# Routing four graphs at once in a fused attention and mixture-of-experts layer, with two PSUM banks for V

## The chip, the cores and the metric

The kernel runs on one core of a Trainium2 chip. The metric is the device time of one execution in microseconds, the median of several. TensorE (PE; its weight loads are listed as PEld), VectorE (DVE), ScalarE (ACT), GpSimd (POOL) and SyncE (SP) each work through their own instructions in order and wait for each other by semaphores; DMAs are issued on SP's, ACT's and POOL's queues.

## The reference

64 graphs of 128 nodes and 512 features each go through one layer: attention with 16 heads and the doubled adjacency as bias, then a mixture of 8 experts of which each node takes its two best.

```python
x = x + attention(layernorm(x), adj, adj, Wq, Wk, Wv, Wo)      # 16 heads, softmax(q k / sqrt(512) + 2 adj) v, Wo
h = layernorm(x)
scores = maximum(h @ gate_W + gate_b, EPS)                      # (64, 128, 8)
p = softmax(scores);  idx = top_k(p, 2)
w = maximum(p, 0.1);  comb = where(in_top_k, w / sum(w[idx]), 0)
y = einsum('bsd,edf->bsef', h, expert_W) + expert_b
x = x + einsum('bsef,bse->bsf', y, comb) / 2
```

## The kernel before

Everything is float32. Projections are made of three matmuls of a rounded high part and the rest as a low part (`three`, L454): high with high, high with low, low with high.

**First phase** (`phase_a`). Loops on all engines run over turns t = -6 to 71 and, in each, over quarters c = 0 to 3. In turn t the attention scores of graph t are made, probabilities of graph t - 1 are transposed, graph t - 2 is multiplied by its values, and graph t - 3 (with t - 2 in odd turns) gets its output projection, residual and second norm. TensorE also makes one big unit of 24 matmuls per quarter (`big`): in even turns Q, Q, V, V for the next pair of graphs, in odd turns O, K, O, K. Units alternate between the banks ps_p[0] and ps_p[1]; V and O have a second, wide half of 264 columns (256 of the projection and 8 gate scores), which goes to ps_g for V (`G_V`) and to ps_m for O (`G_O`). A unit waits until the one before it in its bank has been read: K and Q by VectorE's low parts (L802, L804), V by ScalarE (L654 to L659, which also writes gate_x), O by VectorE's residual (L857 to L859).

**Routing** is made for two graphs at a time, all on 8-element rows, in a chain of small VectorE instructions in which each waits for the one before (`link`): `gate_scores` (turn odd, c = 2), `choose` (odd, c = 3; the two best experts of each node), then in the even turn at c = 1 `weigh` (the weights) and `find_places` (the row of each expert's list that a node gets). Between them TensorE counts nodes with three small matmuls into a corner of ps_g (`G_P`, L595 to L597, even turn, c = 1). Since V's wide half starts the same bank anew, the first V unit of the turn waits for find_places' second instruction (L960, which writes fill). GpSimd then scatters the normalised rows (xn2, four buffers) into the experts' lists x_lists by two indirect DMAs a graph (L1156), one graph a turn, and has the Newton steps of 1/sqrt (`second_rstd`, L1101 to L1111) and the normalising of the probabilities (L1146).

**Transition.** SP loads the experts' weights from turn 61 on, ScalarE rounds them (L755), and VectorE subtracts to get their low parts (`expert_lo`, L974, four instructions of 512 columns for each expert): six at the places of LO_AT between turns 64 and 67, two after the table. The table (L1046 to L1069) lists for each of 135 tiles its expert and its rows, from the counts in fill. All engines meet at the end of the phase.

**Second phase** (`phase_b`): for each tile ScalarE's queue loads 128 rows (L1288), TensorE transposes them and multiplies by the expert's weights (L1260 to L1262), VectorE makes the low part (L1300), adds the bias and scales, and GpSimd adds the rows into out by an indirect DMA (L1343).

## Time and profile before

| | us |
|---|---|
| median of 3 runs (lowest, highest) | 1661.66 (1660.23, 1663.96) |
| the profiled execution | 1662.81 |
| its span in the trace | 1661.0 |
| PE busy, PEld busy | 1550.8, 1410.9 |
| DVE, ACT, POOL busy | 1215.8, 955.9, 974.0 |

The first phase takes the first 1193 us or so, the second the rest. A line of a timeline gives start, duration, engine, line of the kernel, instruction, tile written<-tiles read, shape and count; in brackets stands how long the engine was idle before it and what it was waiting for.

### The profile page before, as it was taken

Reading aid. Unit: us, or ns where it says so; the run is one execution under the profiler, and the core shown is the slowest. Engines: PE = TensorE matmul, PEld = TensorE weight load, DVE = VectorE, ACT = ScalarE, POOL = GpSimd, SP = SyncE. Lnnn points to the kernel's source line nnn. Section 1 sums busy time; section 2 is a strip of 40 time slices with the busy share of each in tenths; the row PEclk is TensorE's granted clock in tenths of the full one; section 3 lists DMA queues with packets and bytes.
Section 4 is the critical chain, followed back from the end, with each engine's and each line's share of the span. In section 5 each row is a group of like instructions: output and inputs, shape, how many; then the busy total and the mean of one; then the engine's idle time right before and its main releaser. Section 6 shows DMA issues by size and latency. Waiting matters only on the chain. (4 is left out here: it accounts for less than half of the span.)

```text
span 1661.0 us, 45460 instructions
## 1 busy us (share of the span) xinstructions
PE 1550.8 (93%) x12808; PEld 1410.9 (85%) x12808; DVE 1215.8 (73%) x4952; ACT 955.9 (58%) x3129; POOL 974.0 (59%) x1788
## 2 busy tenths in 40 slices
PE   6999999999999999999999999966189999999996
PEld 6999999999999999999999999955167777777775
DVE  5578888888888888888888788877745555555554
ACT  4687777777777777777777777775111111111111
POOL 3255666566666666566665666556235565565655
PEclk9999999999999999999999999977599999999998
DMA  6787988789888888888887888794658898898886
GB/s 226 194 233 199 257 241 241 237 248 253 246 241 240 244 247 239 237 239 247 228 244 225 246 233 228 221 293 142 217 102 158 168 174 164 162 169 165 164 160 106
DMA packets 188629, 351.98 MB, mean 212 GB/s; under 512 B 20960, under 2 KB 30304, under 8 KB 188256
## 3 DMA queue, kind: packets, MB, share of 16 engines
q1 hardware_dynamic: 135520, 238.47, 51.7%
q0 software_dynamic: 29680, 69.55, 21.6%
q10 hardware_dynamic: 23184, 41.05, 8.0%
q8 instruction: 109, 1.79, 0.5%
q14 instruction: 136, 1.11, 0.2%
HBM read 189.48 MB, written 159.52 MB: 210 GB/s over the span
## 5 line engine op out<-in xcount | busy, mean ns | idle before, releaser
L678 ACT ACTIVATE prob<-prob,nmax 128x128 f32<-128x128 f32 x1024 | 398.8, 395 | 175.3 <-DVE amax L833 168.8
L1146 POOL TENSOR_TENSOR prob<-prob,rinv 128x512 f32<-128x512 f32 x256 | 261.4, 1042 | 241.3 <-DVE rinv L850 241.2
L829 DVE CUSTOM_DVE_ANT_0 prob<-ps_s,bias 128x128 f32<-128x128 f32 x1024 | 237.7, 287 | 142.1 <-PE ps_s L530 106.5
L1343 POOL DMA_INDIRECT out<-yt,token x135 | 211.6, 1567 | 196.3 <-DMA out<-yt,token 72.3
L1281 ACT ACTIVATE xgT_hi<-ps_x 128x512 fp32r<-128x512 f32 x135 | 80.7, 598 | 386.8 <-PE ps_x L1266 339.4
L1260 PE MATMUL ps_y<-we,xgT_hi 128*128 x540 | 260.8, 483 | 5.8 <-DVE xgT_lo L1300 5.8
L1261 PE MATMUL ps_y<-we,xgT_hi 128*128 x540 | 214.8, 398 | 0.0
L1262 PE MATMUL ps_y<-we,xgT_lo 128*128 x540 | 214.0, 396 | 0.0
L678 ACT ACTIVATION_READ_ACCUMULATOR prob<-prob,nmax 128x1 f32 x1024 | 196.7, 192 | 0.0
L833 DVE TENSOR_REDUCE amax<-prob 128x4 f32<-128x512 f32 x256 | 175.6, 686 | 8.9
L539 PE MATMUL ps_t<-const,prob 128*128 128x128 f32 x1024 | 164.8, 284 | 15.2 <-ACT pT L716 12.1
L1300 DVE TENSOR_TENSOR xgT_lo<-ps_x,xgT_hi 128x512 fp32r<-128x512 f32 x135 | 93.2, 690 | 105.6 <-ACT xgT_hi L1281 102.4
L1266 PE MATMUL ps_x<-const,xg 128*128 128x128 f32 x540 | 147.5, 276 | 21.1 <-DMA xg<-x_lists 21.1
L1156 POOL DMA_INDIRECT x_lists<-xn,pos x128 | 133.6, 1044 | 43.5 <-issue 37.7
L716 ACT ACTIVATE pT<-ps_t 128x512 f32<-128x512 f32 x256 | 152.1, 594 | 11.9 <-PE ps_t L539 9.7
L455 PE MATMUL ps_p<-xT_hi,wk_hi 128*128 128x256 f32 x512 | 150.9, 295 | 1.8 <-DVE xT_lo L815 1.8
L530 PE MATMUL ps_s<-ks,qs 96*128 96x128 f32 x1024 | 145.8, 265 | 7.2 <-issue 4.9
L1260 PEld LDWEIGHTS ps_y<-we,xgT_hi 128*128 128x128 f32 x540 | 102.7, 190 | 56.3 <-issue 9.3
L455 PE MATMUL ps_p<-xT_hi,wq_hi 128*128 128x256 f32 x512 | 149.7, 292 | 0.6 <-DVE kT_lo L802 0.6
L456 PE MATMUL ps_p<-xT_lo,wk_hi 128*128 128x256 f32 x512 | 145.8, 285 | 0.0
L457 PE MATMUL ps_p<-xT_hi,wk_lo 128*128 128x256 f32 x512 | 145.7, 285 | 0.0
L530 PEld LDWEIGHTS ps_s<-ks,qs 96*128 96x128 f32 x1024 | 138.7, 193 | 7.9 <-issue 7.7
(191 smaller groups left out, 4770.4 us busy)
## 6 DMA issues: line engine op xcount, KB each, us to landing
ks<-kq_parts SPq DMA_DIRECT2D x192, 256.0 KB, 4.2
qs<-kq_parts SPq DMA_DIRECT2D x192, 256.0 KB, 6.3
xg<-x_lists ACTq DMA_DIRECT2D x135, 260.5 KB
xin<-x SPq DMA_DIRECT2D x64, 256.0 KB, 7.2
kq_parts<-kT_hi SPq DMA_DIRECT2D x32, 512.0 KB, 3.8
kq_parts<-kT_lo SPq DMA_DIRECT2D x32, 512.0 KB, 4.8
kq_parts<-qT_hi SPq DMA_DIRECT2D x32, 512.0 KB
kq_parts<-qT_lo SPq DMA_DIRECT2D x32, 512.0 KB
```

The source lines that it names most:

```text
L455: mm(out_, lhs_hi, rhs_hi, start=first, stop=False)
L530: last = mm(ps_s[c % 2][:, P * h:P * h + P], qs[:, r, h, c, :], ks[:, r, h, c, :], start=True, stop=True)
L539: last = nc.tensor.transpose(ps_t[:, P * h:P * h + P], prob[:, b % 2, c, h, :], ident)
L678: last = nc.scalar.activation(prob[:, r, c, h, :], prob[:, r, c, h, :], ACT.Exp, bias=nmax[:, r, i:i + 1], scale=-1.0, accum_out=rsum[:, r ...
L716: nc.scalar.activation(pT[:, c].rearrange("p h t -> p (h t)"), ps_t[:, :], ACT.Copy).then_inc(pT_done, 1)
L829: last = nc.vector.tensor_tensor_reduce(out=prob[:, r, c, h, :], in0=ps_s[c % 2][:, P * h:P * h + P], in1=bias[:, b % 4, :], scale=-1.0, s ...
L833: nc.vector.tensor_reduce(amax[:, r, HC * c:HC * c + HC], prob[:, r, c, :, :], axis=AX.X, op=ALU.max, apply_absolute_value=True).then_inc( ...
L1146: tt(prob[:, r, q], prob[:, r, q], rinv[:, r, HC * q:HC * q + HC].unsqueeze(2).to_broadcast([P, HC, P]), ALU.mult)\
L1260: nc.tensor.matmul(ps_y[r][:, :], xgT_hi[:, r, c, :], hi, start=c == 0, stop=False)
L1261: nc.tensor.matmul(ps_y[r][:, :], xgT_hi[:, r, c, :], lo, start=False, stop=False)
L1262: last = nc.tensor.matmul(ps_y[r][:, :], xgT_lo[:, r, c, :], hi, start=False, stop=c == DC - 1)
L1343: pool.indirect_dma_start(out=out, out_offset=bass.IndirectOffsetOnAxis(ap=token[:, m, :], axis=0), in_=yt[:, r, :], in_offset=None, compu ...
```

## The change

Routing works on groups: fourteen of four graphs (0 to 55), then four of two (56 to 63). All its tiles grow from two to four graphs. The steps move: with `last` the last graph of the group, gate_scores at turn last + 3, c = 3; choose at last + 4, c = 0; ScalarE's exponential at last + 4, c = 1; the counting matmuls (`places`) and weigh at last + 4, c = 2; `combine` (the end of the old weigh) and find_places at last + 5, c = 0. For groups of four last + 3 is even. The two V units get a bank each: the first puts its wide half into ps_o, between the multiplications by v of two turns, the second into ps_g. xn2 has eight buffers instead of four, gate_x six instead of eight, and all_one lies in xn2. The products of Wo with the gate move from ps_o to ps_t, and with them a wait from the first multiplication by v to the first transposes of probabilities. Scatters come two turns later for groups of four; so in turns 62 and 63 two graphs each are scattered. Of the experts' low parts four stand in the last turns, two behind the table, and two in the second phase behind the second tile's low part; a table row first_need tells TensorE for the first three tiles which low parts it must wait for.

```diff
+LATE = 6
+GROUPS = [(4 * q, 4) for q in range((B - 8) // 4)] + [(b, 2) for b in range(B - 8, B, 2)]
+LAST_OF = {b + n - 1: g for g, (b, n) in enumerate(GROUPS)}
...
-        G_V, G_P = ps_g[:, 0:D // 2 + E], ps_g[:, 3 * P:3 * P + 3 * E]
+        G_V, G_P = [ps_o[:, 0:D // 2 + E], ps_g[:, 0:D // 2 + E]], ps_g[:, 3 * P:3 * P + 5 * E]
-        O_W, O_S = ps_o[:, 0:DC * E], ps_o[:, DC * E:DC * E + E]
+        O_W, O_S = ps_t[:, 0:DC * E], ps_t[:, DC * E:DC * E + E]
...
-        LO_AT = {0: (B, 0), 1: (B, 2), 2: (B + 1, 0), 3: (B + 2, 0), 4: (B + 2, 2), 5: (B + 3, 0)}
+        LO_AT = {0: (B, 0), 1: (B, 2), 2: (B + 1, 0), 3: (B + 2, 0)}
...
-                    if 2 * n + part:
-                        pe.wait_ge(v_done, 2 * n + part)
-                    if part == 0 and okp((t - 6) // 2):
-                        pe.wait_ge(place_step, PLACE * ((t - 6) // 2) + 1)
+                    if part == 0 and ok(t - 2):
+                        pe.wait_ge(oT_done, t - 1)
+                    if part == 1 and n >= 1:
+                        pe.wait_ge(v_done, 2 * n)
+                    if part == 1 and t - 5 in LAST_OF:
+                        pe.wait_ge(place_step, PLACE * LAST_OF[t - 5] + 1)
...
+                    if b % 2 and ok(b + 3):
+                        pe.wait_ge(v_done, b + 4)
...
+            def places(g):
+                first, n = GROUPS[g]
+                pe.wait_ge(route_step, ROUTE * g + 16)
+                pe.wait_ge(v_done, min(B, first + n + 6))
+                if g >= 1:
+                    pe.wait_ge(place_step, PLACE * (g - 1) + 1)
...
+                mm(rows(G_P, 0, n + 1), tri[:, :], rows(sums, 0, n + 1), start=True, stop=False)
+                for i in range(1, n):
+                    mm(rows(G_P, i + 1, n + 1), ones[:, :], rows(sums, 1, n + 1 - i), start=False, stop=False)
+                for i in range(n):
+                    last = mm(rows(G_P, 0, 1), ones[:, :], rows(sums, i + 1, i + 2), start=False, stop=i == n - 1)
...
-                if b >= 4:
-                    act.wait_ge(scattered[b % 4], 32 * (b // 4))
+                if b >= 8:
+                    act.wait_ge(scattered[b % 8], 32 * (b // 8))
...
-                    p = (t - 6) // 2
-                    if not odd and okp(p):
-                        if c == 1:
-                            weigh(p)
-                            find_places(p)
-                    p = (t - 5) // 2
-                    if odd and okp(p):
-                        if c == 2:
-                            gate_scores(p)
-                        if c == 3:
-                            choose(p)
+                    if c == 3 and t - 3 in LAST_OF:
+                        gate_scores(LAST_OF[t - 3])
+                    if c == 0 and t - 4 in LAST_OF:
+                        choose(LAST_OF[t - 4])
+                    if c == 2 and t - 4 in LAST_OF:
+                        weigh(LAST_OF[t - 4])
+                    if c == 0 and t - 5 in LAST_OF:
+                        combine(LAST_OF[t - 5])
+                        find_places(LAST_OF[t - 5])
...
+            ts(first_need[:, :], tab_f[:, 0, 0:RING], float(DC), float(DC), ALU.mult, ALU.add)
...
-            for e in range(len(LO_AT), E):
+            for e in range(len(LO_AT), LATE):
                 expert_lo(e)
...
-                    if c == (3 - 2 * a if t < B else 3) and okp(p):
-                        scatter(p, a)
+                    if c == (3 if t >= B or not odd else 1):
+                        for b in range(B):
+                            g, a = GROUP_OF[b]
+                            if t == GROUPS[g][0] + GROUPS[g][1] + 4 + a:
+                                scatter(b)
...
+                        if not t.after(R):
+                            need = pe.value_load(v["first_need"][0:1, bass.ds(t.count(), 1)], min_val=DC, max_val=DC * E)
+                            pe.wait_ge(v["we_lo_done"], need)
...
+                    if (g, j) == (0, 0):
+                        for e in range(LATE, E):
+                            for i in range(DC):
+                                hi, lo = (we[:, (2 * e + part) * DC * D + D * i:(2 * e + part) * DC * D + D * i + D] for part in range(2))
+                                tt(lo, lo.bitcast(f32), hi.bitcast(f32), ALU.subtract).then_inc(v["we_lo_done"], 1)
```

The order of three places, with the semaphores that an instruction waits for. First TensorE at the first V unit of turn 34, where the halves meet (ps_p the first half, ps_g or ps_o the wide one), before:

```order
L455 MATMUL ps_p<-wv_hi,xT_hi 128x256
L456 MATMUL ps_p<-wv_lo,xT_hi 128x256
L457 MATMUL ps_p<-wv_hi,xT_lo 128x256
L455 MATMUL ps_g<-wv_hi,xT_hi 128x264 [waits place_step,v_done]
L456 MATMUL ps_g<-wv_lo,xT_hi 128x264
L457 MATMUL ps_g<-wv_hi,xT_lo 128x264
```

and after:

```order
L466 MATMUL ps_p<-wv_hi,xT_hi 128x256
L467 MATMUL ps_p<-wv_lo,xT_hi 128x256
L468 MATMUL ps_p<-wv_hi,xT_lo 128x256
L466 MATMUL ps_o<-wv_hi,xT_hi 128x264 [waits oT_done]
L467 MATMUL ps_o<-wv_lo,xT_hi 128x264
L468 MATMUL ps_o<-wv_hi,xT_lo 128x264
```

The wide half has left the bank that the counts lie in, and waits for oT_done instead of place_step and v_done; place_step is now waited for by the second V unit of every other even turn.

Second, VectorE in turn 34 from the end of quarter 1 (amax is the last instruction of the maxima; qT_lo and xT_lo are low parts; den and what follows is weigh), before:

```order
L833 TENSOR_REDUCE amax<-prob 128x4 [waits s_read]
L804 SCALAR_TENSOR_TENSOR qT_lo<-ps_p,qT_hi 128x256 [waits q_hi_done]
L804 SCALAR_TENSOR_TENSOR qT_lo<-ps_p,qT_hi 128x256
L815 TENSOR_TENSOR xT_lo<-ps_m,xT_hi 128x512 [waits xT_hi_done]
L928 TENSOR_REDUCE den<-eexp 128x2 [waits gexp_done]
L929 TENSOR_TENSOR em<-eexp,mask 128x16
L930 RECIPROCAL wgt<-den 128x2 [waits route_step]
L931 TENSOR_REDUCE e<-em 128x2
```

and after:

```order
L859 TENSOR_REDUCE amax<-prob 128x4 [waits s_read]
L830 SCALAR_TENSOR_TENSOR qT_lo<-ps_p,qT_hi 128x256 [waits q_hi_done]
L830 SCALAR_TENSOR_TENSOR qT_lo<-ps_p,qT_hi 128x256
L841 TENSOR_TENSOR xT_lo<-ps_m,xT_hi 128x512 [waits xT_hi_done]
L855 ISA prob,nmax<-ps_s,bias 128x128 [waits pT_full,s_full]
L855 ISA nmax 128x1
```

Behind xT_lo came the 18 instructions of weigh and find_places; now the maxima of quarter 2 (ISA prob,nmax) follow at once.

Third, VectorE in turns 66 and 67 (pos is the end of find_places for graphs 60 and 61, we the experts' low parts, score the start of the last routing), before:

```order
L964 TENSOR_REDUCE posf<-place_k 128x4 [waits place_step]
L968 CAST pos<-posf 128x4 [waits scattered1,scattered0,place_step]
L974 TENSOR_TENSOR we<-we 128x512 [waits we_hi_done,place_step]
L974 TENSOR_TENSOR we<-we 128x512 x3
L974 TENSOR_TENSOR we<-we 128x512 [waits we_hi_done]
L974 TENSOR_TENSOR we<-we 128x512 x3
L884 SCALAR_TENSOR_TENSOR score<-gate_sum,shift,gate_x 128x8 [waits rstd2_step]
```

and after:

```order
L984 TENSOR_REDUCE posf<-place_k 128x2x2 [waits place_step]
L988 CAST pos<-posf 128x2x2 [waits scattered6,scattered5,scattered7,scattered4,place_step]
L994 TENSOR_TENSOR we<-we 128x512 [waits we_hi_done,place_step]
L994 TENSOR_TENSOR we<-we 128x512 x3
L915 SCALAR_TENSOR_TENSOR score<-gate_sum,shift,gate_x 128x8 [waits rstd2_step]
```

The low parts of two experts stood between the end of find_places and the last scores; one expert's is left there.

## Rows read from the trace of the kernel before

**Rows 1.** Stretches: us, busy of PE, PEld, DVE, ACT, POOL, clock, DMA.
```profile
400.00:600.00 200.00, 199.01 (x1952) 192.58 (x1951) 167.63 (x820) 157.10 (x550) 130.93 (x258) 1.00 0.87 249
...
1185.00:1190.00 5.00, 0.00 (x0) 0.00 (x0) 4.76 (x12) 0.00 (x0) 0.00 (x0) 0.50 1.03 325
```

**Rows 2.** Timeline (start us, us, engine): first V matmul, turns 2, 4, 8, 58.
```profile
86.83 0.36 PE L455 MATMUL ps_p<-wv_hi,xT_hi 128*128 128x256 f32 x1
...
119.84 0.36 PE L455 MATMUL ps_p<-wv_hi,xT_hi 128*128 128x256 f32 x1
...
188.75 0.36 PE L455 MATMUL ps_p<-wv_hi,xT_hi 128*128 128x256 f32 x1
...
1043.06 0.36 PE L455 MATMUL ps_p<-wv_hi,xT_hi 128*128 128x256 f32 x1
```

**Rows 3.** Timeline, TensorE's weight loads at the two V units of turn 34.
```profile
634.13 0.19 PEld L456 LDWEIGHTS ps_p<-wv_lo,xT_hi 128*128 128x128 f32 x1
...
634.26 0.19 PEld L457 LDWEIGHTS ps_p<-wv_hi,xT_lo 128*128 128x128 f32 x1
...
634.54 0.19 PEld L455 LDWEIGHTS ps_g<-wv_hi,xT_hi 128*128 128x128 f32 x1
...
637.73 0.19 PEld L455 LDWEIGHTS ps_p<-wv_hi,xT_hi 128*128 128x128 f32 x1 [0.38 <-DVE qT_lo L804]
...
639.44 0.19 PEld L455 LDWEIGHTS ps_g<-wv_hi,xT_hi 128*128 128x128 f32 x1 [0.24 <-ACT gate_x L659]
```

**Rows 4.** Timeline, VectorE in turn 34: routing, then the low part of q.
```profile
631.72 0.16 DVE L928 TENSOR_REDUCE den<-eexp 128x2 f32<-128x16 f32 x1
...
634.27 0.15 DVE L960 TENSOR_TENSOR fill<-ps_g,fill 128x8 f32<-128x8 f32 x1
...
636.93 0.74 DVE L804 SCALAR_TENSOR_TENSOR qT_lo<-ps_p,qT_hi 128x256 fp32r<-128x256 f32 x2
```

**Rows 5.** Timeline, ScalarE in turn 34: first exponential of quarter 2.
```profile
637.05 0.40 ACT L678 ACTIVATE prob<-prob,nmax 128x128 f32<-128x128 f32 x1 [2.82 <-DVE amax L833]
```

**Rows 6.** Timeline, VectorE: choice (turn 33), residual and scores (turn 35).
```profile
623.78 0.14 DVE L904 TENSOR_TENSOR eq<-score,m 128x16 f32<-128x16 f32 x1
...
625.82 0.21 DVE L916 TENSOR_TENSOR mask_sum<-mask 128x16 bf16<-128x16 f32 x1
...
646.62 0.29 DVE L829 CUSTOM_DVE_ANT_0 prob<-ps_s,bias 128x128 f32<-128x128 f32 x1 [2.42 <-PE ps_s L530]
...
648.85 0.16 DVE L859 TENSOR_TENSOR gate_x<-ps_m,gate_x 128x8 f32<-128x8 f32 x1
...
652.89 0.36 DVE L884 SCALAR_TENSOR_TENSOR score<-gate_sum,shift,gate_x 128x8 f32<-128x8 f32 x2
...
654.11 0.18 DVE L893 TENSOR_TENSOR dlt<-score,m 128x16 f32<-128x16 f32 x1
```

**Rows 7.** Timeline, TensorE in turn 35: first matmul of the second O unit.
```profile
650.39 0.36 PE L455 MATMUL ps_p<-wo_hi,oT_hi 128*128 128x256 f32 x1
```

**Rows 8.** Timeline, VectorE from the last routing into the second phase.
```profile
1167.42 4.91 DVE L974 TENSOR_TENSOR we<-we 128x512 fp32r<-128x512 f32 x8
...
1172.25 0.36 DVE L884 SCALAR_TENSOR_TENSOR score<-gate_sum,shift,gate_x 128x8 f32<-128x8 f32 x2
...
1179.11 0.16 DVE L1032 CAST ends<-fill 1x8 int32<-1x8 f32 x1
...
1206.97 0.69 DVE L1300 TENSOR_TENSOR xgT_lo<-ps_x,xgT_hi 128x512 fp32r<-128x512 f32 x1 [5.63 <-ACT xgT_hi L1281]
```

**Rows 9.** Timeline, GpSimd: a scatter in turn 63, the last rstd2 in turn 66.
```profile
1128.23 1.01 POOL L1156 DMA_INDIRECT x_lists<-xn,pos  x1 [0.15 <-issue]
...
1162.11 0.59 POOL L1107 TENSOR_TENSOR nwt<-var,rstd 128x1 f32<-128x1 f32 x1 [0.18 <-POOL rstd L1106]
...
1164.68 0.19 POOL L1111 TENSOR_TENSOR off<-nmu,rstd 128x1 f32<-128x1 f32 x1 [0.18 <-POOL rstd L1110]
```

**Rows 10.** Timeline, ScalarE's queue: first loads of the second phase.
```profile
1194.29 4.61 ACTq L1288 DMA_DIRECT2D xg<-x_lists  x5
```

More of the change, by code:

```diff
@@ L886, in gate_scores @@
                 link(last)
-                for r in range(2):
+                for r in range(n):
                     last = nc.vector.scalar_tensor_tensor(out=score[:, r, :], in0=score[:, r, :], scalar=rstd2[:, k + r:k + r + 1],
@@ L946, in find_places @@
-            def find_places(p):
-                step = [0]
-                def link(ins):
-                    step[0] += 1
-                    ins.then_inc(place_step, 1)
-                    dve.wait_ge(place_step, PLACE * p + step[0])
-                r = p % 2
-                old, new = fill[:, r, :], fill[:, 1 - r, :]
-                places = G_P.rearrange("p (a e) -> p a e", a=3)
-                dve.wait_ge(place_full, p + 1)
-                tt(place[:, :, :], places[:, 0:2, :], old.unsqueeze(1).to_broadcast([P, 2, E]), ALU.add)
-                link(tt(new, places[:, 2, :], old, ALU.add))
+                link(ts(score[:, 0:n, :], score[:, 0:n, :], GATE_EPS, None, ALU.max))
@@ new lines, in landed, with combine @@
+            def landed(graphs):
+                for b in graphs:
+                    dve.wait_ge(scattered[b % 8], 32 * (b // 8 + 1))
+            def combine(g):
+                first, n = GROUPS[g]
+                link = chain(ROUTE * g, 22, route_step)
+                link(nc.vector.scalar_tensor_tensor(out=wgt[:, :, 0:n], in0=wgt[:, :, 0:n], scalar=1.0 / K,
+                                                    in1=wtot[:, 0:n].unsqueeze(1).to_broadcast([P, K, n]), op0=ALU.mult, op1=ALU.mult))
+                link(tt(comb_k[:, :, 0:n, :], mask[:, :, 0:n, :], wgt[:, :, 0:n].unsqueeze(3).to_broadcast([P, K, n, E]), ALU.mult))
+                landed(range(max(0, first - 8), first - 8 + n))
+                k = first % 8
+                tt(xn2[:, k:k + n, D + 1:W], comb_k[:, 0, 0:n], comb_k[:, 1, 0:n], ALU.add)
+                link(nc.vector.tensor_copy(xn2[:, k:k + n, D], const[:, C_TOK + first:C_TOK + first + n]))
@@ new lines, in find_places @@
+            def find_places(g):
+                _, n = GROUPS[g]
+                link = chain(PLACE * g, 0, place_step)
+                r = g % 3
+                old, new = fill[:, g % 2, :], fill[:, 1 - g % 2, :]
+                places = G_P.rearrange("p (a e) -> p a e", a=5)
+                dve.wait_ge(place_full, g + 1)
+                tt(place[:, 0:n, :], places[:, 1:n + 1, :], old.unsqueeze(1).to_broadcast([P, n, E]), ALU.add)
+                link(tt(new, places[:, 0, :], old, ALU.add))
@@ L961, in find_places @@
                 for k in range(K):
-                    last = tt(place_k[:, k], place[:, :, :], mask[:, k], ALU.mult)
+                    last = tt(place_k[:, k, 0:n], place[:, 0:n, :], mask[:, k, 0:n], ALU.mult)
                 link(last)
-                link(nc.vector.tensor_reduce(posf[:, :, :], place_k[:, :, :, :], axis=AX.X, op=ALU.add))
-                if p >= 2:
-                    for a in range(2):
-                        dve.wait_ge(scattered[2 * (p % 2) + a], 32 * (p // 2))
-                link(nc.vector.tensor_copy(pos[:, r], posf[:, :, :]))
+                link(nc.vector.tensor_reduce(posf[:, :, 0:n], place_k[:, :, 0:n, :], axis=AX.X, op=ALU.add))
@@ L970, in expert_lo @@
+                if g >= 3:
+                    before, m = GROUPS[g - 3]
+                    landed(range(before, before + m))
+                link(nc.vector.tensor_copy(pos[:, r, :, 0:n], posf[:, :, 0:n]))
             def expert_lo(e):
@@ L1195, in _ @@
                         first_rstd(p)
-            for k in range(4):
-                pool.wait_ge(scattered[k], 32 * (B // 4))
+            for k in range(8):
+                pool.wait_ge(scattered[k], 32 * (B // 8))
 def phase_b(nc, v):
```

199 lines of the change are left out of this document (94 added, 105 removed).

## The prediction

> **What bounds the kernel now.** I read the stretches first. Between 400 and 600 us TensorE is busy 199.0 of 200 us at the full clock, while VectorE has 167.6 and ScalarE 157.1 [rows 1]. So the first phase runs at TensorE's pace, and only what stops its stream is worth time. Matmul ends are modelled, so a short stop hardly shows in the busy share; the starts show it. The reader is to take the same matmul, the first of a V unit, pair after pair [rows 2]. Before the first routing a pair of graphs takes 119.84 - 86.83 = 33.01 us. With routing, 25 pairs take 1043.06 - 188.75 = 854.31 us, that is 34.17 each: 1.16 us more.
>
> TensorE's own rows tell where those 1.16 us go [rows 3]. Inside a unit weight loads follow each other by 0.12 to 0.13 us (634.13 to 634.26). At the wide half of the first V unit the step is 634.54 - 634.26 = 0.28. The second V unit starts late, idle 0.38 until VectorE's low part of q; its wide half is idle 0.24 until ScalarE has read gate_x. VectorE's rows say why [rows 4]: weighing and placing of a pair begin at 631.72, the fill count that TensorE awaits is written at 634.27, and the low part of q, queued behind, comes at 636.93. ScalarE's exponentials start 2.82 us late for the same reason [rows 5], and its read of V stands behind them. So one lump of routing on VectorE, at quarter 1 of every even turn, causes all three stops.
>
> At the end of the first phase VectorE is the bound: it subtracts for two experts from 1167.42, starts the last routing at 1172.25, counts the fill at 1179.11, builds the table, subtracts for two more experts, and the second phase's first loads are issued at 1194.29 [rows 8, 10]. After that TensorE has the say again, and the change leaves that part as it is.
>
> **Term 1, the stops in the pairs.** Each V unit of a pair now has a bank of its own, so the wide half of the second waits for a read of the pair before. The fill that frees G_P is written at quarter 0 and wanted at quarter 3, three units of 24 matmuls at 0.12 us (2.9 us each) later. And quarter 1 of the even turn carries no routing at all. What should stay of the 1.16 us is the cost of the placing matmuls. I add up what is lost at the V units over the 28 pairs from turn 6 on, each start less the same step in turns 2 and 4, where there is no routing yet: wide half of the first 5.1 us and the step behind it 2.2, start of the second 12.0, its wide half 5.2 and behind it 2.9, together 27.4 us or 0.98 per pair. The two ways agree if the remaining 0.18 of the 1.16 is the placing matmuls and the restart behind them. I take 27.
>
> Waits that are already met should cost nothing: the same wide half of V with the same wait on v_done, in turns 2 and 4, is within those 33.01 us.
>
> **Term 2, matmuls added.** Fourteen groups of four issue 8 small matmuls, four groups of two issue 4: 128 instead of 96. Before, three of them with the restart cost at most the 0.18 us a pair left over above; If one more costs 0.03 us (an estimate from that 0.18, most of which is the restart), it is 14 x 0.33 + 4 x 0.21 = 5.5 us against 32 x 0.18 = 5.8: nothing. Were each of the 32 more a full weight step of 0.12 [rows 3], it would be 4 us, the other end of the bound. The Trainium skill (TensorE: Matmul & The Clock Gate, on small matmuls) states a floor of about 25 ns from start to start, which would give the same sum.
>
> **Term 3, where VectorE's routing lands now.** Choosing costs 625.82 + 0.21 - 623.78 = 2.25 us and scores 1.40 for two graphs [rows 6]. A column costs (0.61 - 0.18) / (512 - 16) = 0.9 ns, by the low parts of two experts (4.91 us for 8, [rows 8]) and the last score link [rows 6], so 16 more are 0.015 us a link. Four graphs make the choice about 2.4 and the scores, with four instructions more of 0.18, about 2.15. Scores go to quarter 3 of an even turn, choosing to quarter 0 of the next. There the maximum of quarter 1 stood idle 2.42 us for TensorE [rows 6]: the choice fits in almost exactly. Scores push quarter 0 about 0.8 us later. Behind stands the residual, whose last read is 648.85 + 0.16 = 649.01, and TensorE wants that bank at 650.39 [rows 6, 7]: 1.4 us of room less 0.8 leaves 0.4 to 0.6. So I cost it at 0 to 0.5 us a group of four, 0 to 7 us in all, and take 1. Weighing (8 links of 2.25 / 11 = 0.2, 1.6 us) falls at quarter 2 of odd turns, where scores of 1.40 stood before.
>
> The wait for gate_sum moves to the first transposes of probabilities, one turn earlier; a whole V unit of TensorE lies between, and the price is 0. Scatters keep one graph a turn, two turns later, and xn2 has eight buffers for it.
>
> **Term 4, the transition.** Only four low parts stay in front of the last routing. It waits then for the last rstd2, 1164.68 + 0.19 [rows 9], instead of 1172.25: up to 7.3 us earlier. The table has one more instruction, 0.2 us. Two low parts stand behind it as before. The last two go behind the second tile of the second phase, where VectorE idles until 1206.97 and needs 8 x 0.61 = 4.9 us [rows 8]: hidden. Padding is the rival for the end of the phase; DMA is full from 1185 to 1190 [rows 1], but padding is issued on the fill count, which moves as well. Against the 7.1 us: the two graphs' delay of the scatters is caught up in turns 62 and 63, each with two more indirect DMAs of 1.01 us on GpSimd [rows 9], ahead of the rstd and the last normalising. Some of it lies in GpSimd's idle time; I take 1 us, bounds 0 and 2. Two of these also come while keys of the last graph are awaited from full DMA queues: 0 to 1.6 us, I take 0.5. And the first two experts' subtractions now run beside GpSimd's last normalising. Beside such a subtraction a small GpSimd instruction took 0.59 us, and 0.19 without [rows 9]; two to four such steps make 0 to 1.5 us, I take 0.6. Left: 5 us, bounds 2 and 7.
>
> The Trainium skill (SBUF — State Buffer, on the shared port pair) states that a VectorE instruction with two SBUF inputs locks GpSimd out for its whole length, and that descriptors of GpSimd's DMAs can starve. That speaks against low parts in the second phase. By it each of GpSimd's instructions there would wait up to one 0.61 us subtraction. The trace bears the rule out: the 0.59 against 0.19 us of [rows 9] is of that size, but GpSimd has nothing queued between the first tiles' token copies and the first scatter-add, so the sum stays the same.
>
> **Sum.** 27 - 1 + 5 = 31 us. Against the profiled execution (1662.81 us, of which 1661.0 is span) that is 1631.8; the median of the runs shown, 1661.66, is 1.15 lower, and from it comes 1630.7. I say 1630.5.
>
> **Rivals.** (a) The residual comes late in the turns with a choice, by 0.5 to 1 us in each of 14 groups: 7 to 14 us back, 1637 to 1644. For it: room of half a microsecond only, estimated. Against: VectorE is early in that turn, since quarter 1 before it is empty. (b) The transition gives nothing, since GpSimd's doubled scatters or the DMA queues end last: 1635.5. For it: DMA at its full share in two stretches. Against: every one of them starts on something that also moves. (c) The change doesn't do what it says: TensorE's stops come from the wait as such, and a wide half with two waits stays at 0.28. Then 10 to 15 us stay, 1641 to 1646. Against: turns 2 and 4. (d) Slower: scores and choice of four graphs, one behind the other on VectorE, hold up residual and maximum so far that TensorE loses over 31 / 14 = 2.2 us in each such group. That needs links of four graphs to cost half as much again (0.3 us instead of 0.2 for 19 links, 1.9 us) and the low part of k, next in the queue, to be late too; at 3 us a group it is 1642 + 30 = about 1672. The 0.9 ns a column worked out above speaks against: it gives 0.02 us, not 0.1.
>
> **Chances.** Forecast 1626 to 1634: 0.60. (a) 0.15. (b) 0.12. (c) 0.07. (d) 0.03. Something unseen that ends within 0.2% (about what a measurement can tell from no change, 3.3 us): 0.03. The range leaves out the upper part of (c) and the tails, and takes in (a) and (b): 1624 to 1643. Faster by over 0.2% is all but (d) and the unseen: 0.94, same 0.03, slower 0.03.
>
> **What would show it.** Right: a pair of graphs takes about 33.2 us, the V units' loads step 0.12 at their wide halves, no row at the second V unit names qT_lo or gate_x; the second phase's first loads come about 31 us earlier than 1194. Term 3 is wrong if TensorE's second O unit of every other odd turn has an idle time put down to VectorE's gate_x. Term 4 is wrong if from the last residual to the first load of the second phase it is still some 36 us. Wrong altogether if 34.2 us a pair stay.

## The result, and the profile after

The changed kernel takes 1675.47 us (median of 4 runs, 1670.76 to 1679.36) against 1662.47 us (4 runs, 1660.23 to 1663.96) for the kernel before, measured beside it: 1.0078 times as long, 95% interval 1.0049 to 1.0107. Forecast were 1630.5 us, with 1624 to 1643 as the range. The change makes the kernel 13 us slower where 31 us faster were forecast.

The profiled execution of the changed kernel took 1670.76 us, the lowest of its four, with a span of 1668.9; so between the two profiles there are 7.9 us of the 13. The stretch from 400 to 600 us first, beside [rows 1]; the columns are the same:

```profile
400.00:600.00 200.00, 194.88 (x1952) 191.19 (x1950) 161.07 (x721) 156.91 (x544) 128.46 (x255) 1.00 0.86 242
```

TensorE is busy 194.9 of 200 us, where it had 199.0. VectorE has less to do than before (161.1 against 167.6), and still TensorE stands more. The first matmul of the V units of turns 2, 6 and 58 (timeline; start us, us, engine), beside [rows 2]:

```profile
86.46 0.37 PE L466 MATMUL ps_p<-wv_hi,xT_hi 128*128 128x256 f32 x1
...
152.61 0.37 PE L466 MATMUL ps_p<-wv_hi,xT_hi 128*128 128x256 f32 x1
...
1056.09 0.37 PE L466 MATMUL ps_p<-wv_hi,xT_hi 128*128 128x256 f32 x1
```

The two unrouted pairs take 66.15 us, as before. From turn 6 to turn 58 it is 903.48 us, 69.50 for each group of four turns; before, two pairs took 68.34. Turn 58 is reached 13.0 us later than in [rows 2]. The pairs alternate: one of each two takes 33.1 us, as if nothing were routed, the other 34.8 to 38.3.

What TensorE waits for between 200 and 1050 us (view of the waits: us in total, times, longest) has two entries that count:

```profile
PE ps_p L466 <- DVE gate_x L885: 17.2, 13, 1.7
PE ps_p L466 <- DVE qT_lo L830: 10.8, 8, 1.8
```

In the kernel before the same view has 3.8 us for qT_lo and 0.3 for the fill count. A group of four turns takes 69.50 us here and 66.5 where TensorE waits for nothing (experiments 3 and 6); over 850 us that makes about 36 us, and the two waits are 28 of them. The first entry is the second O unit of the turn with the choice, which awaits the residual's read of its bank. The second is the first V unit of the next turn, which awaits the low part of q. One group shows both. First the choice in turn 31, on VectorE, beside [rows 6]:

```profile
579.70 0.17 DVE L876 SCALAR_TENSOR_TENSOR rinv<-amax,rinv 128x8 f32<-128x8 f32 x1
579.79 0.18 DVE L929 TENSOR_TENSOR eq<-score,m 128x32 f32<-128x32 f32 x1
...
580.24 0.19 DVE L931 TENSOR_REDUCE kmax<-key 128x4 f32<-128x32 f32 x1
580.46 0.69 DVE L932 TENSOR_TENSOR mask<-key,kmax 128x32 f32<-128x32 f32 x1
581.19 0.97 DVE L933 SCALAR_TENSOR_TENSOR score<-mask,score 128x32 f32<-128x32 f32 x1
582.19 0.19 DVE L934 TENSOR_REDUCE m<-score 128x4 f32<-128x32 f32 x1
582.41 1.00 DVE L935 TENSOR_TENSOR eq<-score,m 128x32 f32<-128x32 f32 x1
583.44 0.33 DVE L936 TENSOR_TENSOR key<-eq,const 128x32 f32<-128x32 f32 x1
...
584.25 0.19 DVE L941 TENSOR_TENSOR mask_sum<-mask 128x32 bf16<-128x32 f32 x1
...
586.89 0.16 DVE L885 TENSOR_TENSOR gate_x<-ps_m,gate_x 128x8 f32<-128x8 f32 x1
```

GpSimd and TensorE at the same time:

```profile
580.05 2.06 POOL L1166 TENSOR_TENSOR prob<-prob,rinv 128x512 f32<-128x512 f32 x2 [0.26 <-DVE rinv L876]
582.07 1.29 POOL L1203 TENSOR_TENSOR oT_lo<-oT,oT_hi 128x512 fp32r<-128x512 f32 x1
583.32 0.40 POOL L1208 TENSOR_TENSOR bias<-bias 128x128 f32<-128x128 f32 x1
...
587.19 0.36 PE L466 MATMUL ps_p<-wo_hi,oT_hi 128*128 128x256 f32 x1 [1.28 <-DVE gate_x L885]
```

The choice spans 579.79 to 584.44, that is 4.65 us; forecast were 2.4. Seven of its eleven instructions take the 0.2 us that were reckoned with. The other four take 0.69, 0.97, 1.00 and 0.33, and each of them ends 0.05 to 0.07 us behind an instruction of GpSimd: 581.15 and 582.16 behind the two products (580.05 + 1.03 = 581.08 and 580.05 + 2.06 = 582.11), 583.41 behind oT_lo (583.36), 583.77 behind the bias (583.72). Reductions, which read one tile, stay at 0.19 in the middle of it, at 582.19. And it is VectorE itself that lets GpSimd go: the products are released by the rinv at 579.70, the instruction just ahead of the choice.

The kernel before has one such meeting too, in the routing of turn 34, between the rows of [rows 4]. An instruction of weighing, whose neighbours take 0.15 to 0.17 us, takes 0.58 and ends at 632.38, behind GpSimd's subtraction (632.34):

```profile
631.80 0.58 DVE L929 TENSOR_TENSOR em<-eexp,mask 128x16 f32<-128x16 f32 x1
...
631.04 1.30 POOL L1183 TENSOR_TENSOR oT_lo<-oT,oT_hi 128x512 fp32r<-128x512 f32 x1
```

Second, placing in turn 32 on VectorE, and TensorE's first V unit:

```profile
599.44 1.95 DVE L982 TENSOR_TENSOR place_k<-place,mask 128x32 f32<-128x32 f32 x2
601.43 0.22 DVE L984 TENSOR_REDUCE posf<-place_k 128x8 f32<-128x64 f32 x1
601.68 0.94 DVE L988 CAST pos<-posf 128x8 int32<-128x8 f32 x1
...
605.38 0.39 PE L466 MATMUL ps_p<-wv_hi,xT_hi 128*128 128x256 f32 x1 [1.43 <-DVE qT_lo L830]
```

GpSimd has the same products from 599.31 on for 2.04 us and oT_lo from 601.31 for 1.29. Combining and placing span 598.35 to 602.62, 4.27 us; so it is, within 3.9 to 4.3 us, in twelve of the fourteen groups of four.

The transition went as forecast. The fill count is cast at 1186.73 and the first loads go out at 1202.04:

```profile
1186.73 0.16 DVE L1050 CAST ends<-fill 1x8 int32<-1x8 f32 x1
...
1202.04 3.55 ACTq L1313 DMA_DIRECT2D xg<-x_lists  x4
```

From the first V matmul of turn 58 to the cast it is 130.64 us against 136.05 ([rows 2, 8]), and to the first loads 145.95 against 151.23 ([rows 2, 10]), 5.3 us less.

### The profile page after: what moved, and what is told of

Its sections match the earlier page's. It is cut to its first block and busy times, and to the rows that moved or that the text cites. A ratio compares the mean times of both kernels' runs of the same rounds, so it can differ in the third digit from the quotient of the medians.

```text
span 1668.9 us, 45005 instructions
## 1 busy us (share of the span) xinstructions
PE 1540.0 (92%) x12840; PEld 1412.7 (85%) x12840; DVE 1203.5 (72%) x4505; ACT 966.3 (58%) x3115; POOL 973.4 (58%) x1788
## 3 DMA queue, kind: packets, MB, share of 16 engines
q14 instruction: 132, 1.08, 0.2%
## 5 line engine op out<-in xcount | busy, mean ns | idle before, releaser
L555 PE MATMUL ps_t<-const,prob 128*128 128x128 f32 x1024 | 164.9, 284 | 15.7 <-ACT pT L741 10.1
L1339 DVE TENSOR_TENSOR yt<-ps_y,e_bias 128x512 f32<-128x512 f32 x135 | 93.4, 692 | 72.0 <-DMA out<-yt,token 45.9
```

Source lines behind the costliest of these rows:

```text
L555: last = nc.tensor.transpose(ps_t[:, P * h:P * h + P], prob[:, b % 2, c, h, :], ident)
```

## The experiments

Each quoted passage is what was expected, written down before the run. **Theory A**: VectorE's instructions with two operands in SBUF stand while a tensor_tensor of GpSimd runs, so the choice and the placing cost about twice their bare length where the change puts them, and TensorE pays. **Theory B**: four graphs at once are simply too long a lump for these quarters. **Theory C**: it is the order on VectorE, not GpSimd. All times below are medians; the difference is to the kernel before on the same chip, and in brackets stand the ratio of the two and its 95% interval. Waits are TensorE's between 200 and 1050 us, from one profiled execution of each kernel.

**1. The choice ahead of the step that releases GpSimd.** In the same quarter, two steps change places:

```
+                    if c == 0 and t - 4 in LAST_OF:
+                        choose(LAST_OF[t - 4])
                     if c == 0 and ok(t - 1):
                         inverse_sums(t - 1, 1)
...
-                    if c == 0 and t - 4 in LAST_OF:
-                        choose(LAST_OF[t - 4])
```

> The kernel after, with one edit: in the odd turn of the choice, choose stands ahead of inverse_sums of the graph before, in the same quarter, so its eleven instructions run before VectorE gives GpSimd its two normalising products. Theory A (the price of the choice is the wait of VectorE's two-operand instructions while GpSimd's own tensor_tensor runs: in the kernel after 3 of the 11 take 0.69, 0.97 and 1.00 us against 0.19 of the others, so the choice spans 4.65 us): the choice spans at most 2.6 us here, TensorE's second O unit of that turn no longer waits 1.28 us for gate_x, the wait of the first V unit for qT_lo (1.4 to 1.8 us) stays. A group of four turns then takes 69.5 - 1.3 = 68.2 us, and 12 groups give 1675 - 16 = 1659 us. Theory B (the length of the choice itself, in front of the residual, is what costs, whatever its instructions wait for): the residual is as late as before or at most 1 us earlier, the O unit still waits over 0.5 us, 1668 to 1675 us. Against both: GpSimd gets its products 2.4 us later, so TensorE's transposes of the probabilities may wait instead.

Measured: 1639.42 us, 23.9 less than before (0.9847, 0.9828 to 0.9865). The choice, and GpSimd's release:

```profile
568.20 0.20 DVE L929 TENSOR_TENSOR eq<-score,m 128x32 f32<-128x32 f32 x1
...
568.88 0.19 DVE L932 TENSOR_TENSOR mask<-key,kmax 128x32 f32<-128x32 f32 x1
569.10 0.19 DVE L933 SCALAR_TENSOR_TENSOR score<-mask,score 128x32 f32<-128x32 f32 x1
...
570.45 0.19 DVE L941 TENSOR_TENSOR mask_sum<-mask 128x32 bf16<-128x32 f32 x1
...
571.26 2.04 POOL L1166 TENSOR_TENSOR prob<-prob,rinv 128x512 f32<-128x512 f32 x2 [2.76 <-DVE rinv L876]
```

It spans 2.44 us, which is the forecast's length for four graphs. No wait for gate_x is left, and the wait for qT_lo fell too, from 10.8 to 2.3 us:

```profile
PE ps_p L466 <- DVE qT_lo L830: 2.3, 4, 0.7
```

The gain is over twice what I expected (1659), because the V unit's wait was mostly the late choice turn passed on: combining and placing, with their place untouched, now span 4.0 to 4.3 us in only six of the fourteen groups and 2.7 in the others, and each wait for qT_lo stands in a group with a long one. B falls: the lump has its full length here and costs little. That GpSimd starts 2.5 us later costs TensorE nothing that the view shows.

The same turn shows how much room there is: the residual's last read ends at 573.49, and TensorE's second O unit starts 1.10 us later, without a wait.

```profile
573.33 0.16 DVE L885 TENSOR_TENSOR gate_x<-ps_m,gate_x 128x8 f32<-128x8 f32 x1
574.59 0.39 PE L466 MATMUL ps_p<-wo_hi,oT_hi 128*128 128x256 f32 x1
```

**2. The choice or the placing in another quarter.** Three kernels: the choice in quarter 1, behind the residual; combining and placing in quarter 1 of the even turn; both.

```
-                    if c == 0 and t - 4 in LAST_OF:
+                    if c == 1 and t - 4 in LAST_OF:
                         choose(LAST_OF[t - 4])
...
-                    if c == 2 and t - 4 in LAST_OF:
+                    if c == 3 and t - 4 in LAST_OF:
                         weigh(LAST_OF[t - 4])
```

(The placing matmuls of TensorE move from quarter 2 to 3 in the same way.)

> The kernel after, with choose one quarter later (odd turn, quarter 1, behind the residual), the small placing matmuls of TensorE from quarter 2 to quarter 3 and weigh from quarter 2 to quarter 3 of the same turn. Both theories A and B: the residual comes some 4.6 us earlier, TensorE's second O unit stops waiting for it, the wait of the first V unit for qT_lo stays: 1675 - 16 = 1659 us. Theory A adds that the choice is shorter than 4.65 us there if GpSimd's products don't fall into it. If TensorE still waits there, neither holds.

```
-                    if c == 0 and t - 5 in LAST_OF:
+                    if c == 1 and t - 5 in LAST_OF:
                         combine(LAST_OF[t - 5])
                         find_places(LAST_OF[t - 5])
```

> The kernel after, with combine and find_places one quarter later (even turn, quarter 1 instead of 0). In the kernel after they span 4.27 us in quarter 0, where the two place_k products take 1.95 us and the cast of pos 0.94 beside GpSimd's tensor_tensor. Theory A: in quarter 1 GpSimd's large products are over, they span 2.6 us or less; the first V unit stops waiting for qT_lo (1.4 to 1.8 us in each group), the O unit's wait of 1.28 stays: 12 groups by 1.5 us, 1675 - 18 = 1657 us. Rival: the V unit waits because this turn follows the late choice turn, not because of the lump; then its wait stays over 1 us and the time over 1668. A danger: the second V unit waits for the first step of find_places; if that shows, the gain is smaller.

> Both edits together: choose behind the residual in quarter 1 of the odd turn with the placing matmuls and weigh in quarter 3, combine and find_places in quarter 1 of the even turn. If the two lumps on VectorE are all that keeps a group of four turns at 69.5 us instead of the 66.2 of unrouted turns plus 0.4 for the placing matmuls, a group takes 66.6 us and the run 1675 - 12.5 x 2.9 = 1639 us, below the 1662 of the kernel before. If something else holds TensorE, over 1650.

Measured: 1657.26 (6.0 less than before), 1656.41 (6.9 less) and 1641.31 us (22.0 less), with 1659, 1657 and 1639 expected. Alone, the choice behind the residual takes 2.44 us and the wait for gate_x is gone, but the choice now pushes the low part of k, which costs 7.3 us in 12 times, and the qT_lo wait stays (11.6). With both moved, the low part of k is all that is waited for (8.0 us in 13 times). The placing moved alone spans 2.18 us (its two products 0.29 together, its cast 0.17) and removes the qT_lo wait entirely, while the other entry stays as it was:

```profile
PE ps_p L466 <- DVE gate_x L885: 17.2, 13, 1.7
```

**3. The two best edits together**, choice first and placing in quarter 1:

> choose_first with combine and find_places one quarter later in the even turn. In choose_first TensorE still waits 2.3 us in all for qT_lo, and the two place_k products and the cast of pos still take 0.72 and 0.64 us beside GpSimd's products. Theory A: they go to 0.3 and 0.17 us and those waits vanish: 1639 - 2 = 1637 us. Rival: the second V unit waits for find_places now: 1640 or more.

Measured: 1636.66 us, 28.2 less than before (0.9832, 0.9816 to 0.9849), as expected. TensorE waits for nothing between 200 and 1050 us, and a group of four turns takes 66.53 to 66.63 us from turn 10 on. Against the changed kernel, by the two ratios, the two edits are worth 0.0246, that is 41 us.

**4. GpSimd held instead.** VectorE's order stays that of the changed kernel; GpSimd alone gets a wait:

```
+                    if c == 0 and t - 4 in LAST_OF:
+                        hold(route_step, ROUTE * LAST_OF[t - 4] + 16)
                     if c == 0 and ok(t - 1):
                         normalise(t - 1, 1)
```

> The kernel after with its VectorE order untouched (choose behind inverse_sums); one wait is added on GpSimd: in the turns with a choice it starts the two normalising products of quarter 0 only when the choice has ended. Theory A (VectorE's two-operand instructions wait while GpSimd's tensor_tensor runs): the eleven instructions of the choice take 0.16 to 0.20 us each, the choice 2.4 to 2.6 us in place of 4.65, the waits for gate_x vanish, and the time is that of choose_first, 1639 us, within 4 us. Rival C (choose_first was faster because of the order on VectorE, the choice no longer waiting behind inverse_sums for the exponentials): the choice is short but the time stays over 1655 us.

Measured: 1648.88 us (1642.69 to 1650.25), 13.1 less than before. The choice stands where the change put it, behind inverse_sums, and spans 568.68 to 571.11, 2.43 us, with GpSimd's products behind it:

```profile
569.35 0.19 DVE L932 TENSOR_TENSOR mask<-key,kmax 128x32 f32<-128x32 f32 x1
...
571.38 2.04 POOL L1166 TENSOR_TENSOR prob<-prob,rinv 128x512 f32<-128x512 f32 x2 [2.71 <-DVE mask_sum L941]
```

This is the cleanest answer to what lengthens the choice: the order on VectorE is untouched, only GpSimd is out of the way, and the gate_x wait is gone. So C falls as the cause of the stretched choice and of most of the time: holding GpSimd brings 26.6 us of the 36.1 that the exchange of steps brings. But the time missed my 4 us: it is 9.5 over choose_first in median, with 7.4 us of waits for qT_lo in 9 times against 2.3 in 4. Those waits go with the placing, which spans over 4 us in eleven of the fourteen groups here and in six of choose_first. Why it meets GpSimd's products more often isn't settled, so a share of the order in these 9.5 us isn't excluded. The profile is of the fastest execution (1642.69), only 1.7 us over that of choose_first, and says nothing of the rest.

**5. Is it the collision, or the lateness it makes?** choose_first, with ten reductions nobody uses where the changed kernel has its choice:

```
+                    if c == 0 and t - 4 in LAST_OF:
+                        pad = chain(10 * LAST_OF[t - 4], 0, pad_step)
+                        for _ in range(10):
+                            pad(nc.vector.tensor_reduce(kmax[:, :], key[:, :, :], axis=AX.X, op=ALU.max))
```

> choose_first, with ten chained reductions of one operand (0.19 us each with 0.03 to 0.04 between, 2.25 us together, results used by nobody) where the kernel after has its choice, in the same turns. VectorE then reaches the residual as late as in the kernel after, with no instruction waiting for GpSimd. If only the time that VectorE loses counts, whatever it loses it to, the wait for gate_x is back at about 1.3 us and the run near the kernel after: 1668 to 1676 us. If the collision with GpSimd costs something of its own (GpSimd slowed too, its products late), the run stays well below: 1640 to 1660 us.

Measured: 1675.68 us, 13.8 more than before (1.0086, 1.0069 to 1.0103): the changed kernel's time to 0.1%. The choice isn't stretched (2.45 us in the turn shown), VectorE's residual is as late, and TensorE's wait for it is the same:

```profile
582.35 2.17 DVE L1046 TENSOR_REDUCE kmax<-key 128x4 f32<-128x32 f32 x10
...
587.26 0.36 PE L467 MATMUL ps_p<-wo_hi,oT_hi 128*128 128x256 f32 x1 [1.29 <-DVE gate_x L886]
```

So the choice's collision costs what any 2.2 us of VectorE's time ahead of the residual cost; it matters only because it takes them. The padded kernel isn't free of collisions, though, as I had expected it to be. Its placing meets GpSimd's products as in the changed kernel, 4.26 us long in the turn after and around that in twelve of fourteen groups, and the wait for qT_lo is back with it (12.9 us, 10 times):

```profile
599.51 1.96 DVE L983 TENSOR_TENSOR place_k<-place,mask 128x32 f32<-128x32 f32 x2
...
601.75 0.94 DVE L989 CAST pos<-posf 128x8 int32<-128x8 f32 x1
```

The late turn of the choice brings the placing's collision with it; what the placing's would cost by itself, no run separates.

**6. Groups of two.** With GROUPS all pairs, once on choose_first, once on the changed kernel:

```
-GROUPS = [(4 * q, 4) for q in range((B - 8) // 4)] + [(b, 2) for b in range(B - 8, B, 2)]
+GROUPS = [(b, 2) for b in range(0, B, 2)]
```

> choose_first with groups of two graphs throughout instead of four, all else the same (banks, places of the steps, choice ahead of inverse_sums). Theory A: grouping by four is worth only what the shorter work of VectorE and of the placing matmuls is off or on the path; with the choice out of GpSimd's way TensorE waits nowhere, so the time is that of choose_first plus 12.5 extra placings of 0.3 us, 1639 + 4 = 1643 us. Rival: the lumps in every odd turn make VectorE late again, some 1.3 us in each of 12 more turns: 1655 us or more.

> The kernel after with one part undone: groups of two graphs throughout, so a choice in every odd turn, behind inverse_sums as in the kernel after. Theory A: the choice of two graphs meets GpSimd's products just as that of four (the same eleven instructions, each a little shorter), so every pair of turns loses what every group of four loses now, 2 to 3.3 us, in place of every second pair: 12 x 2 to 3.3 us more than the kernel after, 1700 to 1715 us. Rival: the shorter steps of two graphs leave the residual in time; then the time is near 1640 us, and it was the size of the group that cost.

Measured: 1633.54 us with the choice first, 31.3 less than before (0.9806, 0.9788 to 0.9825), and 1680.07 us with the choice where the change has it, 18.1 more (1.0103, 1.0086 to 1.0119). With the choice first four turns take 66.52 us from turn 16 on, so grouping by four is worth nothing once TensorE doesn't wait. It isn't that nothing collides: the placing of two graphs spans 2.7 to 2.9 us in most pairs here and 1.67 with the placing in quarter 1 (the last kernel of experiment 8), but that is in time. With the choice behind inverse_sums the collision is as hard for two graphs:

```profile
587.57 1.08 DVE L932 TENSOR_TENSOR mask<-key,kmax 128x16 f32<-128x16 f32 x1
588.68 0.96 DVE L933 SCALAR_TENSOR_TENSOR score<-mask,score 128x16 f32<-128x16 f32 x1
...
589.88 1.01 DVE L935 TENSOR_TENSOR eq<-score,m 128x16 f32<-128x16 f32 x1
...
PE ps_p L466 <- DVE gate_x L885: 29.5, 24, 1.6
```

(The last line is from its view of the waits.) My 1700 to 1715 was too high all the same: every pair has the wait of 1.2 us, but the V unit's wait of the fours is missing (0.6 us in one place). The placing of two graphs is shorter, 3.05 us against 4.27, which may be why.

**7. The bank alone**, on the kernel before; routing stays by pairs and in its old places:

```
-        G_V, G_P = ps_g[:, 0:D // 2 + E], ps_g[:, 3 * P:3 * P + 3 * E]
+        G_V, G_P = [ps_o[:, 0:D // 2 + E], ps_g[:, 0:D // 2 + E]], ps_g[:, 3 * P:3 * P + 3 * E]
...
-        O_W, O_S = ps_o[:, 0:DC * E], ps_o[:, DC * E:DC * E + E]
+        O_W, O_S = ps_t[:, 0:DC * E], ps_t[:, DC * E:DC * E + E]
...
-                    if 2 * n + part:
-                        pe.wait_ge(v_done, 2 * n + part)
-                    if part == 0 and okp((t - 6) // 2):
+                    if part == 0 and ok(t - 2):
+                        pe.wait_ge(oT_done, t - 1)
+                    if part == 1 and n >= 1:
+                        pe.wait_ge(v_done, 2 * n)
+                    if part == 1 and okp((t - 6) // 2):
                         pe.wait_ge(place_step, PLACE * ((t - 6) // 2) + 1)
...
+                    if b % 2 and ok(b + 3):
+                        pe.wait_ge(v_done, b + 4)
...
+                        pe.wait_ge(v_done, min(B, t + 2))
```

> The kernel before, with one part of the change: the wide half of the first V unit goes to the bank of the attention output (ps_o), that of the second stays in ps_g, with the waits that this needs; routing stays by pairs at its old place. Theory: the prediction's first term, the stops of TensorE in the V units, is due to the shared bank alone: the run is 27 us shorter, 1663 - 27 = 1636 us, and a pair takes 33.3 us in place of 34.17. Rival: part of the 27 us comes back because the first V unit then waits for find_places or for the attention output's reading: 1645 to 1655 us.

Measured: 1654.80 us, 10.1 less than before (0.9944, 0.9928 to 0.9961), 27 expected. Between turns 8 and 58 a pair takes 33.88 us, 0.29 less than in [rows 2]. The time is the rival's, its reason is not: TensorE waits neither for find_places nor for the attention output. With the routing still in quarter 1, the second V unit waits for the low part of q, 10.1 us in all where it was 3.8:

```profile
PE ps_p L455 <- DVE qT_lo L809: 10.1, 25, 0.7
```

**8. The low parts put back**, first on choose_first, then on its version with pairs:

```
-        LO_AT = {0: (B, 0), 1: (B, 2), 2: (B + 1, 0), 3: (B + 2, 0)}
+        LO_AT = {0: (B, 0), 1: (B, 2), 2: (B + 1, 0), 3: (B + 2, 0), 4: (B + 2, 2), 5: (B + 3, 0)}
...
-LATE = 6
+LATE = 8
```

> choose_first with the last low parts of the expert matrices back where the kernel before has them: six in the first phase's last turns, two behind the table, none in the second phase. Theory: the prediction's fourth term, the transition, is worth 5 us (2 to 7): 1639 + 5 = 1644 us. Rival: the transition ends with something else (the scatters of the last pairs), so the time stays at 1639 within 1.5 us; or the low parts in the second phase cost something there and the time falls below 1638.

> pairs_choose_first once more, as the base of the next two on one chip: ratio to the kernel before 0.981, 1633 us.

> pairs_choose_first with the last low parts where the kernel before has them (six in the first phase, two behind the table). If the fourth term is as large as the prediction said, 5 us over pairs_repeat (2 to 7); if the first pair of medians was right, 7.4; if only what the profiled runs show behind turn 58 is real, 2 to 4 us. In all cases the turns before 58 are the same as in pairs_repeat within 0.1 us a pair.

> pairs_choose_first with combine and find_places one quarter later. TensorE waits for nothing between 200 and 1050 us in pairs_choose_first, so there is nothing to win: same within 1.5 us. If the second V unit has to wait for find_places, some 0.3 us a pair, 10 us slower.

Measured: 1646.87 us for the first, 7.4 over choose_first. But its turns 2 to 58, which the edit doesn't touch, take 939.14 us against 935.68, so half of that is nothing of the edit's; in this execution nine of the fourteen placings are long, against six. From turn 58 to the first loads it needs 147.47 us against 143.74. On pairs, side by side on one chip: 1635.18 us (0.9822, 0.98 to 0.9843) for the base, 1634.91 us (0.9835, 0.9813 to 0.9858) with the low parts back, 1631.97 us (0.9814, 0.9792 to 0.9835) with the placing in quarter 1. The three can't be told apart. In the base the second phase's first tile is turned at 1167.06, 145.08 us behind turn 58, and in the other at 1169.57, 148.12 behind it, 3.0 later; but from there to the end the base needs 466.6 us and the other 463.5. The row behind it in the base:

```profile
1171.35 4.89 DVE L1331 TENSOR_TENSOR we<-we 128x512 fp32r<-128x512 f32 x8
1177.46 0.69 DVE L1325 TENSOR_TENSOR xgT_lo<-ps_x,xgT_hi 128x512 fp32r<-128x512 f32 x1 [1.22 <-ACT xgT_hi L1306]
```

The subtractions end 1.2 us before VectorE is wanted again, so they don't stand in the way by themselves. What gives the 3 us back is open: the second phase's length after its first tile varies by 5.1 us among the profiled runs. It is 462.4 to 465.7 us in the four without low parts in it and 463.7 to 467.5 in the twelve with them, so a small cost of theirs there is neither shown nor excluded.

| kernel | us | to before, same chip |
|---|---|---|
| changed kernel | 1675.47 | +13.0 |
| choice first | 1639.42 | -23.9 |
| choice behind the residual | 1657.26 | -6.0 |
| placing in quarter 1 | 1656.41 | -6.9 |
| both of these | 1641.31 | -22.0 |
| choice first, placing in quarter 1 | 1636.66 | -28.2 |
| GpSimd held | 1648.88 | -13.1 |
| choice first, padded | 1675.68 | +13.8 |
| pairs, choice first | 1633.54, 1635.18 | -31.3, -26.2 |
| pairs only | 1680.07 | +18.1 |
| bank only | 1654.80 | -10.1 |
| choice first, low parts back | 1646.87 | -18.0 |
| pairs, choice first, low parts back | 1634.91 | -26.5 |
| pairs, choice first, placing in quarter 1 | 1631.97 | -29.4 |

## Why the prediction was wrong

**What bounds the kernel** held: where TensorE waits for nothing the turns are shortest, and the changed kernel's two waits make most of what it loses. VectorE's busy time (167.6 us before, 161.1 after) pointed the wrong way.

**Term 1** held as a sum. The stops named there are gone in the changed kernel: the weight loads step 0.12 across the first V unit's wide half, beside [rows 3], and the second V unit has no idle time at its start.

```profile
606.66 0.19 PEld L468 LDWEIGHTS ps_p<-wv_hi,xT_lo 128*128 128x128 f32 x1
606.78 0.19 PEld L466 LDWEIGHTS ps_o<-wv_hi,xT_hi 128*128 128x128 f32 x1
...
609.54 0.19 PEld L466 LDWEIGHTS ps_p<-wv_hi,xT_hi 128*128 128x128 f32 x1
```

Where TensorE waits for nothing, four turns take 66.52 us against 68.34, 1.82 less, or 23.7 us over the 13 groups from turn 6 to 58, which is 25 over 28 pairs, with 27 taken. The pair of about 33.2 us was 33.26. I had not said which part brings it: the bank alone brings 10.1 us, and the wait that experiment 7 leaves is for the low part of q, behind the routing of quarter 1. That emptying this quarter brings all the rest wasn't tried by itself.

**Term 2** held: with the choice first and the placing in quarter 1, pairs and fours take 66.52 and 66.54 us for most stretches of four turns.

**Term 3** is the step that failed, and with it the forecast. It took the choice from [rows 6], where it stands at the end of an odd turn with GpSimd's large products not beside it, and moved that price to quarter 0 unchanged: "Four graphs make the choice about 2.4". Its bare length was right (2.44 us in choose_first). But there it stands just behind inverse_sums, which releases two products of 1.03 us each on GpSimd with a subtraction of 1.29 queued behind them, and it became 4.65 us. The room was even larger than the half microsecond reckoned, 1.10 us in choose_first; 2.21 us more of choice than there leave a delay of 1.11, near the 1.28 us that TensorE's row shows. The same with the placing, 4.27 us where 2.18 or less are its length: the forecast gave no price to that at all. Both together cost 41 us (experiment 3), where 1 was taken. The prediction had named this very sign for Term 3 being wrong: an idle time of the second O unit put down to VectorE's gate_x.

The lock was in front of me. The prediction quotes the Trainium skill on VectorE locking GpSimd out, and costs it at the transition alone, with GpSimd as the one that waits. The Trainium skill (SBUF — State Buffer, "SBUF: two separate sides") says that whichever of the two starts first holds the pair and the other blocks for the whole instruction. The trace agrees: 0.69, 0.97 and 1.00 us, each ending with GpSimd's instruction. I weighed the rule where I looked for a price of the low parts, and not in the turns, where it counts 14 times; the 0.58 us of turn 34 in the kernel before stood beside the rows that I read.

**Rivals.** What came is (a) and (d) in one: the mechanism of both, the residual late in the choice turns, at the size of (d), whose "at 3 us a group it is 1642 + 30 = about 1672" is 3.5 us from the result. Its 3 us a group were right as well (69.50 less 66.5), but that is luck: (d) asked for links half as long again and was rejected by the cost of a column; the links didn't grow with the graphs, four of them stood and waited. "Against: VectorE is early in that turn", said of (a), named the room and not what is beside it. (d) had 0.03 of the chance, (a) 0.15. (b) did not come, since the first loads are 5.3 us nearer to turn 58. (c) is refuted by the step of 0.12.

**Term 4** gave the right number in this comparison: from turn 58 to the end of the span the changed kernel needs 612.8 us against 617.9, 5.1 less, with 5 taken. But experiment 8 says that the moved low parts as such are worth 3 us at the start of the second phase and nothing that medians can tell at its end. What the rest of the 5.1 is due to wasn't tried, and that it came to 5 is in part luck. From turn 58 to the first loads the padded kernel, which has the moved low parts too, needs 150.43 us, near the 151.23 of the kernel before, and choose_first 143.74: how late VectorE is in the last turns moves this stretch by more than the low parts do.

**The sum** would have been close without Term 3: 31 us were forecast. Groups of four with choice and placing out of GpSimd's way give 28.2, pairs with the choice first 31.3 and 26.2.

## What to carry to other kernels

Before moving a chain of small VectorE instructions, look up what GpSimd does at the new place, and above all whether the instruction just ahead of the chain is what sets GpSimd going: a price read where GpSimd had only steps of 0.2 to 0.6 us nearly doubled here. If VectorE's step releases a long tensor_tensor on GpSimd, put the small two-operand work ahead of the release when GpSimd's result isn't wanted at once. And when it is a question whether a stretched instruction costs more than its time, pad the good version with harmless instructions of the same length: here that gave the bad version's time to 0.1%. Then look in the padded version's trace whether its other steps are still those of the good one; here the placing's were not.

## What the runs showed of the hardware

- A VectorE instruction with two operands in SBUF that takes 0.17 to 0.19 us took up to 1.08 us beside a tensor_tensor of GpSimd (pairs only, 587.57) and ended with it. Reductions of one operand stayed at 0.19 us, and the maxima of turn 31, which read scores from PSUM and the bias from SBUF, kept their 0.29 us at 592.27 while GpSimd's products ran from 591.71 for 2.04 us. A cast of eight integers a partition is caught too, though it reads one operand only: 0.94 us in the changed kernel, ending at 602.62 behind the subtraction's 602.60, against 0.17 with the placing in quarter 1. So Theory A's "two operands" isn't the whole condition.
- GpSimd is not slowed in return by so small a neighbour: its two products take 2.06 us with the choice beside them and 2.04 without.
